# Early-fusion transformer block on one core: the FFN's row statistics move into the attention stage, both gelu tiles are quantised on ACT, one transfer spreads the softmax denominators

## The reference

```python
h = h + attention(layernorm(h))     # 12 heads of 16, q = k = v, causal by multiplication with the mask
h = h + ffn(layernorm(h))
def rmsnorm(x, g): return x * rsqrt(mean(x * x) + 1e-6) * g
def act_quant(x):                    # per row
    scale = 127 / clip(max(abs(x)), 1e-5, None)
    return clip(round(x * scale), -128, 127) / scale
def bitlinear(x, w, g): return act_quant(rmsnorm(x, g)) @ weight_quant(w).T   # ternary weights
def ffn(x): return bitlinear(gelu(bitlinear(x, w1, g1)), w2, g2)               # 192 -> 768 -> 192
```

## Time and profile before

| | us |
|---|---|
| median of 3 runs (1777.07 to 1780.6) | 1779.1 |
| the profiled execution | 1777.08 |
| its span from first to last instruction | 1775.3 |
| of the span busy: PE / DVE / ACT / POOL | 1531.2 / 1424.0 / 1241.7 / 1108.6 |
| mean granted clock of TensorE, share of 2.4 GHz | 0.883 |

### The profile page before, as it was taken

How to read it: one execution, slowest core, us unless ns; L and a number is a source line. 1 busy time by engine, 2 the same in 40 slices (tenths; PEclk the granted TensorE clock), 3 DMA queues, 4 the chain that set the end, 5 groups by cost and what they waited for, 6 DMA issues and landing times.

```text
span 1775.3 us, 49322 instructions
## 1 busy us (share of the span) xinstructions
PE 1531.2 (86%) x16298; PEld 1246.8 (70%) x16298; DVE 1424.0 (80%) x3227; ACT 1241.7 (70%) x1862; POOL 1108.6 (62%) x1369
## 2 busy tenths in 40 slices
PE   5799999999999999999999999985566667666665
PEld 2678888888888888888888888874455555555554
DVE  5578878787878787878788878863799999999996
ACT  1466666767666666676666666652688888888887
POOL 5456566666666666656565656642677777777775
PEclk8899999999999999999999999996566666666666
DMA  8533333343424243433333333310000000000000
GB/s 203 78 54 62 65 60 66 59 67 55 71 52 73 52 73 52 71 55 68 58 65 61 61 65 60 66 55 18 6 23 24 20 24 20 24 22 22 24 20 28
DMA packets 106240, 93.26 MB, mean 53 GB/s; under 512 B 24785, under 2 KB 96642, under 8 KB 106210
## 3 DMA queue, kind: packets, MB, share of 16 engines
q1 hardware_dynamic: 105442, 91.30, 27.2%
q0 software_dynamic: 768, 1.57, 0.4%
HBM read 73.84 MB, written 11.91 MB: 48 GB/s over the span
## 4 chain that ended last, share of the span: by engine, by line
PE 69%; DVE 16%; issue 6%; ACT 2%; DMA 1%; POOL 1%; DVEq 1%; SPq 1%; ACTq 0%; POOLq 0%
PE ps L1038 20%; PE ps L1095 9%; PE ps L1178 8%; PE ps L1169 7%; PE ps L1125 5%; DVE ff_st L814 5%; PE ps L1157 3%; PE ps L1151 3%; PE ps L1130 3%; PE ps L1277 3%; PE ps L1258 2%; DVE xpix L795 2%; PE ps L1086 2%; DVE xpix L807 2%; PE ps L1076 2%
## 5 line engine op out<-in xcount | busy, mean ns | idle before, releaser
L1038 PE MATMUL ps<-w_eff,pix 124*112 124x193 f32 (+1 forms) x2048 | 406.6, 337 | 11.3 <-DMA pix<-side 8.7
L677 DVE TENSOR_REDUCE nmax<-ps 116x12 bf16<-116x1344 f32 (+2 forms) x192 | 298.7, 1556 | 88.5 <-PE ps L1130 87.3
L493 POOL TENSOR_TENSOR pix<-probs,g_b 112x192 f32<-112x192 f32 (+1 forms) x512 | 296.9, 611 | 110.0 <-ACT probs L993 100.6
L881 ACT ACTIVATE probs<-ps,isw 116x688 f32<-116x688 f32 x384 | 299.1, 831 | 85.4 <-PE ps L1157 84.6
L1038 PEld LDWEIGHTS ps<-w_eff,pix 124*112 124x112 f32 (+1 forms) x2048 | 308.0, 166 | 37.7 <-issue 22.8
L440 POOL TENSOR_SCALAR_AFFINE_SELECT probs<-probs 116x464 f32<-116x464 f32 x384 | 282.3, 748 | 62.5 <-ACT probs L881 54.2
L420 POOL TENSOR_TENSOR xsq<-xsq 124x784 f32<-124x784 f32 (+1 forms) x128 | 184.3, 1440 | 218.5 <-ACT xsq L874 213.5
L863 ACT ACTIVATE pix<-xpix 54x896 f32<-54x896 f32 (+1 forms) x128 | 195.7, 1531 | 0.8
L1247 PE MATMUL ps<-ident_h,xpix 112*96 112x112 f16 (+1 forms) x256 | 35.0, 281 | 158.2 <-DVE xpix L831 158.2
L1258 PE MATMUL ps<-w1t,xpix 96*112 96x384 f16 (+1 forms) x512 | 158.4, 483 | 14.2 <-ACT xpix L984 13.1
L1095 PE MATMUL ps<-xnT,wq_pad 97*128 97x228 f32 (+1 forms) x768 | 166.6, 366 | 0.0
(11 more groups left out here) (134 smaller groups left out, 3138.0 us busy)
## 6 DMA issues: line engine op xcount, KB each, us to landing
xpix<-in_x SPq DMA_DIRECT2D x192, 196.0 KB
rden<-den_rows SPq DMA_DIRECT2D x256, 85.5 KB, 2.1
out<-xpix SPq DMA_DIRECT2D x64, 87.0 KB
out<-xpix SPq DMA_DIRECT2D x64, 84.0 KB
xpix<-in_x SPq DMA_DIRECT2D x128, 34.1 KB
den<-o_sb SPq DMA_DIRECT2D x256, 2.7 KB
h_all<-shift_w SPq DMA_DIRECT2D x5, 768.0 KB, 13.5
pix<-side SPq DMA_DIRECT2D x64, 36.8 KB
```

The source lines that it names most:

```text
L493: last = nc.gpsimd.tensor_tensor(v2[0:P, b, tile, cols], gel[0:P, b, tile, cols], g2_b[0:P, cols], ALU.mult)
L677: V.tensor_reduce(dst, src, AX_X, ALU.max, negate=True).then_inc(s_mx, 1)
L881: A(probs[0:TB, g, 2 * e:2 * e + 2, :], ps[0:TB, 4 + 2 * e:6 + 2 * e, 0:SK], ACT.Exp, scale=isw[0:TB, 7:8]).then_inc(s_p, 1)
L1038: last = MM(ps_tok[tile][0:P, :], pix[0:HI, par, o, lo:lo + P], w_eff[0:HI, o, :], start=(o == 0), stop=(o == OFFS - 1))
```

## The change

- In the attention stage DVE does `measure(n-1)` at the end of step n: `bn_stats`, `bn_aggr`, the variance, a copy of the means, the centred rows and their peak, for the image whose attention was just added. POOL gets `row_roots`, a power of two columns, behind the last `clear_later`.
- Between the stages five DVE instructions on 128 columns make the first quantiser's scales and steps for all images at once.
- In the FFN stage DVE's step keeps the centring, the final add, the gelu peak, `q1` and five small instructions on two columns. `tensor_scalar` and `tensor_tensor` there have become `scalar_tensor_tensor`. The sum of squares is scaled on ACT, and POOL adds epsilon and takes the power in `gelu_roots`, behind the weighting and no longer ahead of it.
- ACT quantises both tiles as before, with a semaphore for each, and PE turns tile 0 after the first of them.
- One DMA with 72 pieces takes the place of four with 18 pieces each.

```diff
-        v1 = part(xpix, 384, 2 * DIM).rearrange("p (t d) -> p t d", t=2)
+        v1 = tok_t
...
-                for j in range(PER):
-                    row = 32 * j + HD
-                    sp.dma_start(den[SPREAD * j:SPREAD * (j + 1), :],
-                                 o_sb[row:row + 1, :, :].rearrange("p g k -> p (g k)")
-                                 .rearrange("p (s k) -> p s k", s=SPREAD)).then_inc(s_den, 16)
+                sp.dma_start(den[:, :], o_sb[HD:128:32, :, :].rearrange("p g k -> p (g k)")
+                             .rearrange("p (s k) -> p s k", s=SPREAD)).then_inc(s_den, 16)
...
+            def row_roots(m):
+                pool.wait_ge(s_var2, m + 1)
+                nc.gpsimd.tensor_tensor(rms[:, bass.ds(m * 2, 2)], ln_st[:, 32:34], expo[:, 0:2],
+                                        ALU.pow).then_inc(s_rms, 1)
...
+                if prev:
+                    row_roots(n - 2)
...
-            def ffn_step(i, b, new=True, mid=True):
-                if new or mid:
-                    pool.wait_ge(f_var, i + 2)
-                    nc.gpsimd.tensor_tensor(ff_st[:, b, 20:24], ff_st[:, b, 16:20], expo[:, 0:4],
-                                            ALU.pow).then_inc(f_r1, 1)
...
+            def weight(n, b):
+                after(pool, f_q2[0], n - 1)
+                after(pool, f_q2[1], n - 1)
+                for tile, P in enumerate((TA, TB)):
+                    pool.wait_ge(f_g, 2 * n + tile + 1)
+                    for lo in range(0, HIDDEN, HIDDEN // 4):
+                        cols = slice(lo, lo + HIDDEN // 4)
+                        last = nc.gpsimd.tensor_tensor(v2[0:P, b, tile, cols], gel[0:P, b, tile, cols],
+                                                       g2_b[0:P, cols], ALU.mult)
+                    last.then_inc(f_v2, 1)
+            def gelu_roots(n, b):
+                pool.wait_ge(f_ssq, 2 * n + 2)
+                apart(pool)
+                nc.gpsimd.tensor_scalar(ff_st[:, b, 18:20], gel_sum[:, b, :], EPS_RMS, None,
+                                        ALU.add).then_inc(f_var, 1)
+                pool.wait_ge(f_var, n + 1)
+                nc.gpsimd.tensor_tensor(ff_st[:, b, 20:22], ff_st[:, b, 18:20], expo[:, 0:2],
+                                        ALU.pow).then_inc(f_r1, 1)
...
-                for k in range(2):
-                    step(V.tensor_copy(w_step[:, 2 * k:2 * k + 2], isw[:, 4 + k:5 + k].to_broadcast([128, 2])))
...
-                dve.wait_ge(s_den, 16 * PER * (n + 1))
+                dve.wait_ge(s_den, 16 * (n + 1))
...
+            def measure(n):
+                def chain(ins, k):
+                    ins.then_inc(s_mean2, 1)
+                    dve.wait_ge(s_mean2, n * 3 + k)
+                dve.wait_ge(s_h2, n + 1)
+                apart(dve)
+                for tile, P in enumerate((TA, TB)):
+                    last = V.bn_stats(ln_st[0:P, 20 + 6 * tile:26 + 6 * tile], h_all[0:P, hcols(n, tile)])
+                chain(last, 1)
+                apart(dve)
+                for tile, P in enumerate((TA, TB)):
+                    last = V.bn_aggr(ln_st[0:P, 34 + 2 * tile:36 + 2 * tile], ln_st[0:P, 20 + 6 * tile:26 + 6 * tile])
+                chain(last, 2)
+                after(dve, s_rms, n)
+                V.tensor_scalar(ln_st[:, 32:34], ln_st[:, 35:38:2], 1.0 + EPS_RMS,
+                                EPS_LN * EPS_RMS, ALU.mult, ALU.add).then_inc(s_var2, 1)
+                V.tensor_copy(mean2[:, bass.ds(n * 2, 2)], ln_st[:, 34:38:2])
+                for tile, P in enumerate((TA, TB)):
+                    last = V.scalar_tensor_tensor(v1[0:P, tile, :], h_all[0:P, hcols(n, tile)],
+                                                  ln_st[0:P, 34 + 2 * tile:35 + 2 * tile], g1_b[0:P, :],
+                                                  ALU.subtract, ALU.mult)
+                chain(last, 3)
+                for tile, P in enumerate((TA, TB)):
+                    last = V.tensor_reduce(peak[0:P, bass.ds(n * 2 + tile, 1)], v1[0:P, tile, :], AX_X, ALU.max,
+                                           apply_absolute_value=True)
+                last.then_inc(s_peak, 1)
...
                     regroup_odd(n + 4, 1 - b, coming)
+                if prev:
+                    measure(n - 1)
...
+            links[:] = [0, IMAGES * V_FRONT]
+            dve.wait_ge(s_peak, IMAGES)
+            dve.wait_ge(s_rms, IMAGES)
+            link(V.tensor_tensor(peak[:, :], rms[:, :], peak[:, :], ALU.mult))
+            link(V.tensor_scalar(peak[:, :], peak[:, :], 1e-5, None, ALU.max))
+            link(V.reciprocal(inv_peak[:, :], peak[:, :]))
+            V.tensor_scalar(step1[:, :], peak[:, :], isw[:, 4:5], None, ALU.mult)
+            link(V.scalar_tensor_tensor(scale1[:, :], inv_peak[:, :], 127.0, rms[:, :], ALU.mult, ALU.mult))
+            dve.sem_inc(f_sc1, 1)
...
+            def centre(n):
+                after(dve, f_q1, n)
+                for tile, P in enumerate((TA, TB)):
+                    ins = V.scalar_tensor_tensor(v1[0:P, tile, :], h_all[0:P, hcols(n, tile)],
+                                                 mean2[0:P, bass.ds(n * 2 + tile, 1)], g1_b[0:P, :],
+                                                 ALU.subtract, ALU.mult)
+                ins.then_inc(f_v1, 1)
+            def quantise_first(n):
+                dve.wait_ge(f_v1, n + 1)
+                after(dve, f_t1, n)
+                for tile, P in enumerate((TA, TB)):
+                    ins = V.scalar_tensor_tensor(q1[0:P, tile, :], v1[0:P, tile, :],
+                                                 scale1[0:P, bass.ds(n * 2 + tile, 1)],
+                                                 magic[0:P, :].to_broadcast([P, DIM]), ALU.mult, ALU.add)
+                ins.then_inc(f_q1, 1)
...
+            def peaks(n, b):
+                dve.wait_ge(f_v2, 2 * n + 2)
+                for tile, P in enumerate((TA, TB)):
+                    ins = V.tensor_reduce(ff_st[0:P, b, 26 + tile:27 + tile], v2[0:P, b, tile, :], AX_X, ALU.max,
+                                          apply_absolute_value=True)
+                flinks[:] = [0, n * F_LINKS]
+                flink(ins)
...
+            def second_scales(n, b):
+                st = ff_st[:, b, :]
+                after(dve, f_q2[0], n - 1)
+                dve.wait_ge(f_r1, n + 1)
+                flink(V.scalar_tensor_tensor(st[:, 28:30], st[:, 20:22], 1.0, st[:, 26:28], ALU.mult, ALU.mult))
+                flink(V.scalar_tensor_tensor(st[:, 28:30], st[:, 28:30], 1e-5, unit, ALU.max, ALU.mult))
+                flink(V.reciprocal(st[:, 32:34], st[:, 28:30]))
+                assert flinks[0] == F_LINKS
+                V.scalar_tensor_tensor(st[:, 42:44], st[:, 28:30], isw[:, 5:6], unit, ALU.mult, ALU.mult)
+                V.scalar_tensor_tensor(st[:, 38:40], st[:, 32:34], 127.0, st[:, 20:22],
+                                       ALU.mult, ALU.mult).then_inc(f_sc, 1)
...
+            def ffn_step(i, b, new=True, mid=True, last_=True):
+                if new:
+                    centre(i + 1)
+                if last_:
+                    final(i - 3, 1 - b)
                 if mid:
-                    dve.wait_ge(f_ssq, 2 * j + 2)
-                    ins = V.tensor_scalar(st[:, 18:20], gel_sum[:, 1 - b, :], 1.0 / HIDDEN, EPS_RMS, ALU.mult,
-                                          ALU.add)
-                if new or mid:
-                    ins.then_inc(f_var, 1)
-                if new:
-                    for tile, P in enumerate((TA, TB)):
-                        ins = V.scalar_tensor_tensor(v1[0:P, tile, :], h_all[0:P, hcols(m, tile)],
-                                                     st[0:P, 12 + 2 * tile:13 + 2 * tile], g1_b[0:P, :],
-                                                     ALU.subtract, ALU.mult)
-                    flink(ins)
-                    for tile, P in enumerate((TA, TB)):
-                        ins = V.tensor_reduce(st[0:P, 24 + tile:25 + tile], v1[0:P, tile, :], AX_X, ALU.max,
-                                              apply_absolute_value=True)
-                if last_:
-                    o = i - 3
-                    dve.wait_ge(f_m2, o + 1)
-                    after(dve, f_out, 32 * o)
-                    for tile, P in enumerate((TA, TB)):
-                        end = V.scalar_tensor_tensor(y[0:P, tile, :], ps[0:P, 1, tile * 256:tile * 256 + DIM],
-                                                     st[0:P, 42 + tile:43 + tile], h_all[0:P, hcols(o, tile)],
-                                                     ALU.mult, ALU.add)
-                    end.then_inc(f_y, 1)
+                    peaks(i - 1, 1 - b)
...
+                if new:
+                    quantise_first(i + 1)
...
+                    second_scales(i - 1, 1 - b)
...
-            def quantise(i, b, tile):
-                P = (TA, TB)[tile]
-                if tile == 0:
-                    act.wait_ge(f_sc, i + 2)
```

(19 more changed lines are left out.)

119 lines of the change are left out of this document (46 added, 73 removed).

## The result

| | before | after |
|---|---|---|
| median of 4 runs, us | 1779.8 (1777.07 to 1780.6) | 1847.4 (1844.02 to 1850.62) |
| ratio, with its 95% interval | | 1.038 (1.036 to 1.040) |
| the profiled execution, us | 1777.08 | 1844.02 |
| its span, us | 1775.3 | 1842.0 |

The change made the kernel 3.8% slower: +67.6 us between the medians, where +41 on the profiled execution was forecast. 1847.4 lies in the range, near its upper end.

A forecast was written before the change was run, and what follows sets the result against it. PE was taken to bound the attention stage, and DVE, with ACT close behind, the FFN stage. Attention +79, FFN -39 and ends +1 made +41 on 1777.1, so 1818 us, range 1784 to 1850.

The forecast's parts named there:

- The ring: Attention stage: DVE and PE hand-overs once round sum to 19.21 us in place of 17.91; 61 steps give +79 us.
- The single transfer: Attention stage: one denominator transfer lands sooner, worth 0.11 us in a steady step and 2.2 us at the stage's end.
- the ends: End of the attention stage: 2.2 us gained by the transfer, against one `measure` and five instructions; sum +1 us.
- The FFN step: FFN stage: DVE no longer bounds, the step falls from 7.92 to 7.3 us; over 63 steps -39 us.
- ACT's floor: FFN stage: ACT's unchanged work, run without a gap, allows no step under 7.05 us.
- PE's turn of `q2`: FFN stage: 1.32 us on PE's path at the lower clock, a path that makes the step 7.79 us.
- Rival 1: Attention stage: `measure` fits into DVE's 3.7 us of idle time, the step stays 17.91 us; 1739 us, chance 0.12.
- Rival 2: Attention stage: PE's new waits let its granted clock fall, adding 183 us; about 2000 us, chance 0.04.
- Rival 3: FFN stage: POOL becomes the bound, pieces 15% longer, step 7.6 us, gain only 19 us; 1838 us, chance 0.12.
- The rule quoted there: FFN stage: GpSimd contends with DVE instructions in two-port mode or with two SBUF inputs, so the new forms disturb POOL.
- Rival 4: FFN stage: PE stays slow, the step is 7.8 us, -8 us in place of -39; 1849 us, chance 0.07.

The follow-up runs named there:

- experiment 5: The changed kernel with four transfers of the denominators again in place of the single one: 1854.8 us, ratio 1.042.
- Experiment 7: The changed kernel with `q1` made right after the centring, ahead of the final add and the gelu peaks, in the FFN step: 1826.3 us, ratio 1.026.
- experiment 4: The changed kernel with `measure` split into four pieces at different places of the attention step, only the peak left at its end: 1758.6 us, ratio 0.988.
- experiment 2: The changed kernel with the second half of `measure` (centring and peak) left out: 1788.9 us, ratio 1.005.
- experiments 8: The changed kernel with `q1` made by `tensor_scalar` in place of `scalar_tensor_tensor`, same order: 1842.7 us, ratio 1.035.
- 11: The changed kernel with `measure` in four pieces, `q1` ahead of the peaks, and the clip and the step by `tensor_scalar`: 1734.7 us, ratio 0.976.

## Why the prediction was right, and where it was off

The sign, the stage and the mechanism were right: `measure` in one piece lengthens a ring that runs from the second maxima over `front` and `q_lo` to PE's values and back. The attention stage lost 14 us more than forecast and the FFN stage gained 14 us less.

**The ring.** Measured over the two kinds of step that alternate (19.19 and 19.81 from one second maxima to the next), against the prediction's terms:

| term | predicted | measured |
|---|---|---|
| second maxima to the end of `regroup_odd` | 5.41 | 5.46 |
| `measure` with its gaps | 2.70 | 2.79 (2.68, 2.90) |
| `front` to the end of `q_lo` | 5.29 | 5.28 (5.09, 5.47) |
| semaphore to PE, values to the next second maxima | 5.81 | 5.97 |
| sum | 19.21 | 19.50 |

Each term held to 0.16. Over 61 steps the 0.29 would make 18 us; the line of `front` shows 14, +93 in place of +79. The largest part is PE's: 0.14 us from the end of `q_lo` to the start of the values (635.98 to 636.12) where I had taken 0.08 from another hand-over, and 5.83 in place of 5.73 behind it. Both could have been read before. I took the start of the values from the critical chain (611.02), where PE's timeline has 610.96. And in the next step of the kernel before it has

```profile
628.93 1.38 PE L1169 MATMUL ps<-probs,vaug 112*32 112x228 f32 x32
```

which is 0.14 behind the end of `q_lo` (628.79) and 5.83 ahead of the next second maxima (634.76). So the half microsecond that `q_lo` seemed to have to spare (610.50, 611.02) was there in about half of the steps only; in the others the spare time was all in the 1.04 before `front`. In the changed kernel the ring closes twice over in the steps where PE does not wait for `q_lo`: `q_lo` ends at 616.17, PE's own work up to the values at 616.28, and they start at 616.32.

**The single transfer** gave 0.015 us a step (experiment 5) where I took 0.11: the last part of that 0.11 was the start of an instruction that overlapped the one before it, and its end came only 0.05 sooner. At the stage's end it gave 2.1 of the predicted 2.2, and the ends came to -1.4, where +1 stood.

**The FFN step** is the term that was mis-sized: 7.52 us where I took 7.3, so -25 in place of -39. I put ACT's floor and PE's turn of `q2` on the path and left out that `q1` now stands behind the peaks and so beside POOL's pieces, which hold its first tile for 2.7 to 3.0 us in 12 of 53 steps. ACT's waits for it come to 0.24 us a step, which is what is missing. Experiment 7 takes `q1` away from there, and the step is 7.29. That 7.3 was right for the rest of the step is in part luck: it was a point a third of the way between two bounds. My figures for DVE were wrong too: "under 75%" was 86%, 6.46 us a step (343.75 of 400 times 7.52) in place of 5.6 or less. Beside POOL's pieces `q1`'s first tile took 1.15 us for 0.41, and the first two small instructions 0.68 and 0.51 where they take 0.16 alone. ACT, said to be above 93%, had 91%.

**Rival 1** (`measure` fits into the idle time) was false for the place that the change chose and true for another: experiment 4 hides all of it. My sentence that the idle time ahead of the second and third maxima "is of no use, since it waits for PE" holds only for work that stands elsewhere. I had put rival 1's threshold at 1.95 us of `measure`; experiment 2 shows that 1.36 us already cost 0.56 a step, and with the FFN's smaller gain that version is slower than the kernel before (1.005).

**Rival 2** is out: PE waited 1.1 to 1.7 us a step (1.09 in one kind, 1.34 and 0.40 in the other), and the stretch's granted clock stayed at 0.99.

**Rival 3** named the right engine and the wrong way. The pieces did grow, by a tenth (0.63 to 0.69) and not 15%, but POOL had 326 of 400 us and 63 us of waits for gelu, so it did not bound. Nor did the longer pieces cost the time: in the steps that were lost they ran on (4.87 us for eight, where 5.33 is usual), and it was `q1` that stood still. The rule quoted there, that two SBUF inputs on DVE disturb GpSimd, is borne out in one order (pieces of 0.69 with `q1` beside them, 0.62 with `q1` out of the way). A form with one input is no remedy, since it is held up as well (experiments 8, 11); the rule names the two-port mode beside the two inputs, so it does not promise one.

**Rival 4** (nothing for the FFN, 1849) is near the total by chance: the FFN gained 25 us, and the attention stage lost the difference.

Still open is what decides whether DVE gets in between two pieces. In the changed kernel's 53 steps, none of the 17 `q1` that began within 0.41 us of POOL's first piece was held; of the 33 that began 0.57 to 0.93 behind it, 12 were, and the other 21 took 0.43 to 0.76. Reversing the order of issue of the two was not tried.

## What to carry to other kernels

Where two engines hand work round a ring, added work costs by its place and not by the engine's load: look for the longest wait for the other engine and put the work directly ahead of it, in pieces no longer than that wait, and leave the stretch that the other engine waits for as short as it was. When a producer for PE is moved behind a reduction that waits for a third engine, look at what that engine does next: the producer now runs beside it and can be held by it; issue it first if its inputs are ready. A mean can hide two kinds of step: when a wait is rare and long, look at the single steps. A saving read as the start of the next instruction can be only an overlap: compare ends.
